# One core, two graph layers in one kernel: another assignment of nodes to partitions, scores stored as columns, and the first node tiles loaded in small pieces

## What is computed

```
# layer 0, a = alpha[0]
A'  = a * adj;  diagonal of A' += 1 - a
deg = A'.sum(axis=1)
x1  = layernorm(x + relu((A' @ x) / deg @ W.T + b))
# layer 1
xt  = x1 * artanh(|x1|) / |x1|                              # logmap0, norms clipped
P   = adj   * sigmoid((xt @ wp[:d])[:, None] + (xt @ wp[d:])[None, :] + bp)
C   = adj.T * sigmoid((xt @ wc[:d])[:, None] + (xt @ wc[d:])[None, :] + bc)
y   = proj(expmap0((C + P) @ xt))
out = layernorm(x1 + y)
```

## Time and profile before

| | before |
|---|---|
| median of three runs | 2200.4 us (2196.5 to 2200.65) |
| the profiled execution's own time | 2200.13 us |
| its span, first to last instruction | 2198.3 us |
| mean granted TensorE clock | 0.98 |
| moved by DMA | 820.37 MB, mean 373 GB/s |
| panel loop (256 pairs, 154 units) | to about 1242 us |
| late units (358) | to about 2177 us |
| end after the last unit | about 21 us |

### The profile page before, as it was taken

How to read it: one execution, slowest core, us unless ns; L and a number is a source line. 1 busy time by engine, 2 the same in 40 slices (tenths; PEclk the granted TensorE clock), 3 DMA queues, 4 the chain that set the end, 5 groups by cost and what they waited for, 6 DMA issues and landing times. The chain is left out here.

```text
span 2198.3 us, 18369 instructions
## 1 busy us (share of the span) xinstructions
PE 2006.2 (91%) x5072; PEld 898.4 (41%) x5072; DVE 1929.8 (88%) x1864; ACT 1318.0 (60%) x1508; POOL 1340.4 (61%) x639
## 2 busy tenths in 40 slices
PE   7999999999999998999999978898888888889886
PEld 3444444444444444444444433343333333334333
DVE  5757787988989989898999989999998998989896
ACT  0001324454464454454453588988989988989996
POOL 0000304534455554644544677999998998999996
PEclk9999999999999999999999988999999999999998
DMA  9978988989989989988989998999999999999993
GB/s 338 362 273 291 400 288 349 406 343 384 388 329 409 414 331 363 392 337 337 416 345 348 422 408 329 421 420 421 422 410 421 421 419 394 421 421 398 398 393 143
DMA packets 128453, 820.37 MB, mean 373 GB/s; under 512 B 14880, under 2 KB 27488, under 8 KB 31328
## 3 DMA queue, kind: packets, MB, share of 16 engines
q1 hardware_dynamic: 113392, 799.06, 90.7%
q10 hardware_dynamic: 14960, 20.13, 2.7%
HBM read 814.88 MB, written 4.26 MB: 373 GB/s over the span
## 5 line engine op out<-in xcount | busy, mean ns | idle before, releaser
L548 POOL TENSOR_TENSOR chi<-chi,ring 128x1024 f32<-128x1024 f32 x326 | 834.4, 2573 | 628.5 <-ACT chi L756 572.4
L1244 PE MATMUL ps<-keys,xtA 128*128 128x512 f32 x2048 | 981.3, 611 | 140.1 <-DVE keys L1045 110.5
L1171 PE MATMUL ps<-ring,xA 128*128 128x512 f32 x2048 | 918.4, 598 | 33.8 <-DMA xA<-in_x_g 15.2
L773 ACT ACTIVATE ps<-scores,prcr 128x1024 f32<-128x1024 f32 x492 | 544.2, 1106 | 394.2 <-DVE keys L1045 377.5
L1244 PEld LDWEIGHTS ps<-keys,xtA 128*128 128x128 f32 x2048 | 377.6, 193 | 683.8 <-issue 653.0
L935 DVE TENSOR_TENSOR dsum<-dsum,ring 128x2048 f32<-128x2048 f32 x240 | 594.1, 2475 | 30.4 <-DMA ring<-in_g_blk 24.4
L1171 PEld LDWEIGHTS ps<-ring,xA 128*128 128x128 f32 x2048 | 387.5, 192 | 519.1 <-issue 493.9
L1045 DVE TENSOR_TENSOR keys<-ps,chi 128x1024 f32<-128x1024 f32 x426 | 521.6, 1225 | 85.6 <-issue 31.3
L756 ACT ACTIVATE chi<-scores,prcr 128x1024 f32<-128x1024 f32 x426 | 483.8, 1136 | 16.3 <-DMA scores<-plcl_d 8.5
L1036 DVE TENSOR_TENSOR ps<-ps,ring 128x1024 f32<-128x1024 f32 x348 | 425.5, 1223 | 44.4 <-ACT ps L773 39.0
L548 POOL TENSOR_TENSOR chi<-chi,xA 128x1024 f32<-128x1024 f32 x79 | 185.7, 2366 | 18.4 <-ACT chi L756 18.4
(11 more groups left out here) (122 smaller groups left out, 820.9 us busy)
## 6 DMA issues: line engine op xcount, KB each, us to landing
ring<-in_g_blk SPq DMA_DIRECT2D x443, 1024.0 KB, 8.6
ring<-in_a_cols SPq DMA_DIRECT2D x190, 1024.0 KB, 10.0
xA<-in_a_cols SPq DMA_DIRECT2D x51, 1024.0 KB, 11.9
xA<-in_g_blk SPq DMA_DIRECT2D x44, 1024.0 KB, 10.0
scores<-in_a_cols SPq DMA_DIRECT2D x15, 1024.0 KB, 11.7
scores<-in_g_blk SPq DMA_DIRECT2D x15, 1024.0 KB, 10.7
scores<-plcl_d ACTq DMA_DIRECT2D x22, 512.0 KB, 10.4
xA<-in_x_g ACTq DMA_DIRECT2D x64, 64.0 KB, 11.8
```

The costliest lines, as they stand in the source:

```text
L548: pool.tensor_tensor(out=chi(n), in0=chi(n), in1=half(t, n), op=ALU.mult).then_inc(m2_ready, 1)
L773: act.activation(dst, scores[:, row, 0, :], ACT.Sigmoid, bias=prcr[:, 2 * jt:2 * jt + 1]).then_inc(p_ready, 1)
L1171: ins = pe.matmul(Y[:, h * BANK:(h + 1) * BANK], xA[:, tile * D:(tile + 1) * D], t[:, tt * BP + h * BANK:tt * BP + (h + 1) * BANK], start= ...
L1244: ins = pe.matmul(outp[:, h * BANK:(h + 1) * BANK], xtA[:, jt * D:(jt + 1) * D], keys(n)[:, h * BANK:(h + 1) * BANK], start=begins, stop=i ...
```

## The change

A partition now holds eight neighbouring nodes of a panel, not two of a pair of tiles. Node p * 8 + k of a panel is in partition p and tile k.

- A 1 MB load takes rows k and k + 1 of each partition's eight. It is still 8 KB in one piece for each partition, but the pieces of neighbouring partitions lie 32 KB apart in DRAM, where they were next to each other.
- `columns(t, k)` has a step of eight values (32 bytes), not two (8 bytes). It is the stationary operand of the degrees, the linear layer, the own turns, the sums of squares and the last transposes.
- `turn_own` writes PSUM contiguously. The DVE product and sum of the 20 own units read PSUM (and the product writes it) with a step of 128 values inside and 8 values in a run.
- `scored` goes to DRAM straight from its 16 columns, 32 bytes a partition and transfer. `row_scores`, `copy_rows` and their semaphores are gone. The store is at tick 21 (the copy was at 23), the load at 23 (was 25), own early units begin at tick 25 (was 27) and `SLOT_THREE` is three units earlier.
- Node tiles: every transfer of `load_nodes` goes to 16 partitions. The first panel's tiles 0 and 1 come by eight pieces of 16 KB (`x_first`), the other six tiles by eight of 48 KB (`x_in[0]`), half of each on ACT's queue, half on SP's behind pairs 0 and 1. The semaphores count whole panels: pair 0 waits for `x_first`, pairs 1 to 3 for `x_in[0]`, pairs 4 to 7 for `x_in[1]`, and so on.
- Stores of results have 4 KB in one piece for each partition (2 KB in the last two).

```diff
-SLOT_TWO, SLOT_THREE = LATE0, LATE0 + 41
+SLOT_TWO, SLOT_THREE = LATE0, LATE0 + 38
...
         def columns(t, k):
-            at = k // 2 * 2 * P + k % 2
-            return t[:, at:at + 2 * P - 1:2]
+            return t[:, k:BP:TPP]
+        def in_turn(t):
+            return t.rearrange("q (k p) -> q p k", k=TPP)
+        def in_order(t):
+            return t.rearrange("q (p k) -> q p k", k=TPP)
...
+        def load_nodes(queue, G, k0, k1, there):
+            r = G // 2
+            for c in range(GT):
+                a = (G % 2 * GT + c) * P // TPP
+                queue.dma_start(xA[a:a + P // TPP, r * BP + k0 * D:r * BP + k1 * D].rearrange("a (k d) -> a k d", d=D),
+                                x_g[G].rearrange("(a k) (c d) -> c a k d", k=TPP, d=D)[c, :, k0:k1, :]).then_inc(there, 16)
...
-                sp.dma_start(out[p * BP:(p + 1) * BP, :].rearrange("(c p t) d -> p c (t d)", p=P, t=2),
-                             x1f[k % 2][:, :].rearrange("p (c e) -> p c e", e=2 * D)).then_inc(out_done, 16)
+                sp.dma_start(out[p * BP:(p + 1) * BP, :].rearrange("(p k) d -> p (k d)", k=TPP),
+                             x1f[k % 2][:, :]).then_inc(out_done, 16)
...
                 if kind == "pair" and j in (2, 4):
-                    sp.wait_ge(x_in[j // 2 - 1], 64)
+                    sp.wait_ge((x_first, x_in[0])[j // 2 - 1], 16 * TPP)
                 wait_free(e, before)
-                sp.dma_start(entry(e), src.rearrange("(p t) c -> p (t c)", t=2)).then_inc(r_in[e], 16)
+                src = blk.rearrange("(p k) c -> p k c", k=TPP)[:, k:k + 2, :]
+                sp.dma_start(entry(e).rearrange("p (t c) -> p t c", t=2), src).then_inc(r_in[e], 16)
+                if kind == "pair" and j < 2:
+                    load_nodes(sp, 1, 2 * j, (2, TPP)[j], (x_first, x_in[0])[j])
...
-            def copy_rows(r):
-                act.wait_ge(rowp_ready, r + 1)
-                act.activation(rows.rearrange("a (p t) -> a t p", t=2),
-                               E[0:TPP, 0:2 * P].rearrange("a (t p) -> a t p", t=2), ACT.Copy).then_inc(rows_ready, 1)
-                act.wait_ge(rows_ready, r + 1)
+            def store_scores(r):
+                act.wait_ge(scored_ready, r + 1)
                 for k in range(2):
-                    act.dma_start(plcl_d[k, r * BP:(r + 1) * BP].rearrange("(c e) -> c e", e=2 * P),
-                                  rows[k * TPP // 2:(k + 1) * TPP // 2, :]).then_inc(rows_out, 16)
+                    act.dma_start(plcl_d[k, r * BP:(r + 1) * BP].rearrange("(p t) -> p t", t=TPP),
+                                  scored[:, k * TPP:(k + 1) * TPP]).then_inc(rows_out, 16)
...
-            load_nodes(0)
-            load_nodes(1)
+            load_nodes(act, 0, 0, 2, x_first)
+            load_nodes(act, 0, 2, TPP, x_in[0])
...
             for G in range(2, NG):
-                load_nodes(G)
+                load_nodes(act, G, 0, TPP, x_in[G // 2])
...
+                if n in OWN_AT:
+                    dve.tensor_tensor(out=in_turn(s), in0=in_turn(s), in1=in_order(other), op=ALU.mult).then_inc(m1_ready, 1)
+                    return
...
+                if n in OWN_AT:
+                    dve.tensor_tensor(out=in_order(keys(n)), in0=in_turn(s), in1=in_order(chi(n)),
+                                      op=ALU.add).then_inc(k_ready, 1)
...
                 if r == 0:
-                    pe.wait_ge(x_in[q // 2], 64)
+                    pe.wait_ge(x_first if q == 0 else x_in[q // 4], 16 * TPP)
...
-            def row_scores(r):
-                pe.wait_ge(scored_ready, r + 1)
-                pe.wait_ge(prcr_ready, r + 1)
-                for t in range(2):
-                    ins = pe.transpose(E[0:TPP, t * P:(t + 1) * P], scored[:, t:2 * TPP:2], ident[:, :])
-                ins.then_inc(rowp_ready, 1)
...
-                    ins = pe.transpose(columns(slots[s], k), columns(half(t, h), UNIT[n][2] % TPP), ident[:, :])
+                    ins = pe.transpose(slots[s][:, k * P:(k + 1) * P], columns(half(t, h), UNIT[n][2] % TPP), ident[:, :])
```

64 lines of the change are left out of this document (24 added, 40 removed).

## The result

The changed kernel takes 2243.1 us (median of four runs, 2237.29 to 2245.05), the kernel before 2199.06 in the same session. The ratio is 1.0197, 95% interval 1.0175 to 1.0219: two per cent slower. The prediction was 2197.6 with a range to 2223; the time lies 20 us above the range.

The account below looks back on a forecast made before the run. PE was taken to bound the first 1242 us, loads the late units. From 2200.1 us, 0 - 1.8 + 0 - 1 + 0.3 = -2.5 gave 2197.6; own range 2191 to 2204, full range 2191 to 2223.

Parts of the forecast that it names:

- Weight loads: PE's stationary operands at a step of eight in the first stage: taken as 0 extra, lower bound 0.
- The upper bound: Each strided weight load takes another 0.12 us: up to 27 us in seven panels, up to 2.9 at the end.
- the first rival: Slower: PE weight loads with one value a line cost up to 30 us; 2212 to 2228, centre 2222; 18%.
- Finals' sums: Sums of squares on PE in the late stage: extra load time hidden behind transfers, PE idle 13%; taken as 0.
- The start: Panel 0: PE begins 3.4 us earlier, pair 4 waits for groups 2 and 3; net taken as 0.
- The hole is gone: Start: the gap in DMA traffic at 10 to 12 us vanishes because SP has already sent pairs 2 and 3.
- SP can send only pairs 2 to 8: Start: DVE waits for the constants before its third pair, so SP then has no free ring entry.
- The second rival: Slower: node-tile transfers to 16 partitions delay pair 4 and panel 0, +5 to +14 us; 2203 to 2212; 12%.
- The transposes of the scores: Two score transposes on PE's path disappear, 0.26 us for each of seven panels: -1.8 us.
- The own products: DVE's strided PSUM reads in 20 own units: mostly hidden, taken as 0, bounds 0 and +8 us.
- The DRAM distance: Pieces of 1 MB loads 32 KB apart cost nothing: taken as 0, bounds -4 and +16 us.
- The scores' path: Direct score store without ACT's copy, rows loaded two ticks later: taken as +0.3 us, bounds 0 and +5.

Follow-up runs that it names:

- d1: Kernel before, only the sums of squares read their stationary operand with a step of eight instead of two: 2210.58 us (1.0061).
- c5: c1 with the sums of squares also reading contiguous stationary operands: 2206.74 us (1.003).
- c1: Changed kernel with the stationary operands of degrees and linear layer read in one contiguous piece of 128 columns: 2218.35 us (1.0085).
- c2: Kernel before, with a step of eight in the degrees and the linear layer only: 2226.85 us (1.0124).
- e1: Kernel before, step two throughout, with the eight matmuls of the sums of squares issued twice: 2216.25 us (1.0073).
- c3: Changed kernel with node tiles loaded and waited for by half panels, so pair 4 waits for four tiles: 2236.13 us (1.0168).
- d3: Changed kernel with the eight node transfers of panel 1 moved ahead of the nine constants on ACT's queue: 2238.88 us (1.0182).
- c7: Changed kernel, x in node order with whole-panel tile transfers; degrees' and linear layer's operands written in tile order, read contiguously: 2200.61 us (1.0008).
- c8: c7 with ACT also writing the squares in tile order, so the sums of squares read contiguous operands: 2191.21 us (0.9961).
- d2: c8, but ACT reads the squares' source with a step of eight and writes in one piece: 2191.09 us (0.9965).

## Why the prediction was wrong, step by step

**Weight loads: the step that failed first.** "I take 0, since step two, already half the data of each access, cost so little." Step two costs 6 ns a load, step eight 126: nothing of the second could be read from the first. The upper bound, a load that takes its own 0.12 us again, was what happened to within 5%, and the first rival's mechanism was the true one, with its sign, sixteen matmuls "at 3 us or more" (3.73). It had 18%. With the row of step two alone as evidence, and a rule that named just this change as the border, the two should have been about even.

**Finals' sums: hidden, it said.** Of these 128 loads only the last sixteen, at the end, were in the upper bound; the 112 among the units were in none, because PE is idle 13% late. The question was not whether PE has room but who waits for these sums, and what is queued behind the one who waits. The timeline of before had the answer: at the first final the ACT instruction that takes them starts 0.1 us after PE is through (1476.85 + 1.93 = 1478.78, ACT at 1478.89), so nearly all of the 1.8 us more is a wait of ACT, with the sigmoids behind it. Where the margin was 0.8 us, ACT waits 0.7 to 1.0. Cost: 11 us, by d1 and c5 alike.

**The clock** was in no term. It costs 1.7 us behind the degrees of panel 1 and about 3 after the long wait of panel 0, and beyond that at most a few us: the loads and ACT's wait alone explain the differences of c1, c2, d1 and e1 to within 2 or 3.

**The start.** PE's first matmul was forecast at 6 to 7 us, it came at 7.36. Then two premises failed. "The hole is gone": it was there. And "SP can send only pairs 2 to 8": that needs constants which land late, and ACT's queue had reached them at 4.5 us, 1.6 earlier than before; six of them used the hole, the last landed at 22.2, and SP sent two loads more. The forecast 31.6 to 33.5 became 42.14. In c3, where the constants did land late and DVE held SP, the whole of panel 1 had landed at 35.0, near the forecast: the arithmetic of turn-taking was sound, and it was the order of events that was wrong. The second rival (tiles through few partitions) had the bill right, +5 to +14 against 12.0, but by luck as far as the changed kernel goes: its sign, PE idle on node tiles after 45 us, is not there. Its reckoning of a panel that needs more than PE's 110 us fits what d3 shows at pair 24. It had 12%.

**What held.** The transposes of the scores are gone, and step eight costs transposes no more than step two did. The own products take 1221 ns, as before. The DRAM distance costs nothing. The scores' path and `SLOT_THREE` show no cost: units 154 to 195 take 131.9 us in both. After the loads are taken out, panels 1 to 7 take less than before the change: 1104.7 to 1110.0 us in c1, c5, c7, c8 and d2, 1109.8 to 1112.5 in the kernel before, d1 and e1. Some 1.8 us of that are the two transposes; the rest is not clear of what traces differ by.

**The range.** The measured +42 us of the span is the first rival's 25, the second's 12 and the 11 that had been declared hidden, less some 6: 4.6 in panels 1 to 7, where traces differ by as much, and 1.3 between panel 7 and unit 154. Each rival was priced alone, on top of an otherwise unchanged sum, so the range ended at 2223, at the centre of the first. They don't exclude each other: with 18% and 12%, both together was a case, at 2197.6 + 25 + 12 = 2235, and it was in no sum.

## What to carry to other kernels

When a change alters the stride of an operand, look for a row with that stride, in that kind of instruction, before pricing it; if there is none, the doubling is as likely as nothing, and the engines that write the operand may be able to turn it for next to nothing (here DVE and POOL could, ACT at twice the time). Idle time of an engine hides nothing that another engine is waiting for: find the instruction that takes the result, the margin it has now (here 0.1 to 0.8 us), and what is queued behind it. Many small transfers on one queue beside large ones on another cost by their number, and here reordering them only moved the wait; count how many of them the waiting engine needs before it can start; add up independent rivals before the range is closed.

## What the runs showed of the hardware that had not been expected

- A stationary operand with a step of 32 bytes costs 238 ns a matmul record against 118 at a step of 8 bytes in an ordinary float32 matmul, but no more in a transpose (weight load 187 ns against 209; 141 contiguous).
- Blocks of small matmuls of 3.7 to 5 us on PE, with step eight or without, were joined in many places by 3.4 or 6.8 us at a granted clock of 0.50, which began 2 to 5 us after the start of the block: at six of the seven finals before the last in the changed kernel, five in d1, seven in e1. Blocks of 1.9 us at the same places were not, in the kernel before and in c5. At the last final the clock fell in every one of these runs.
- ACT takes 2.0 to 2.1 us for 1024 values with a step of 32 bytes on either side, 1.04 without. DVE (PSUM read, 1277 to 1280 ns against 1275 to 1280) and POOL (write, 2373 against 2352) hardly notice it.
- Transfers of 16 partitions and 64 KB, several in flight and nearly alone on the DMA, moved 147 to 191 GB/s at a DMA share of 0.9.
